# Layer norm kept feature-major, with sums over partitions as f32 matmuls against ones, in an eight-core macaron block on Trainium2

## What is computed

```python
x = x + 0.5 * tanh(layernorm(x) @ W @ A1 @ A2 + bias)
u = layernorm(x)
q, k, v = u @ Wq + bq, u @ Wk + bk, u @ Wv + bv
Q, K = elu(q) + 1, elu(k) + 1
KV, Ksum = sum(K * v, axis=1), sum(K, axis=1)      # over the sequence
V = Q * KV / (Q * Ksum + 1e-6)
x = x + gelu(V @ Wo + bo)
x = x + 0.5 * tanh(layernorm(x) @ W @ A1 @ A2 + bias)
```

## Time and profile before

| quantity | us |
|---|---|
| median of two runs | 3260.82 |
| lowest, highest | 3228.44, 3293.2 |
| profiled execution, its own time | 3213.7 |
| span on its slowest core (core 2) | 3212.1 |
| spans of the eight cores | 3197.8 to 3212.1 |
| mean granted TensorE clock, dies 0 and 1 | 0.790, 0.805 |

### The profile page before, as it was taken

The page is one execution under the profiler, slowest core; times in us unless marked ns, Lnnn a source line. Parts: engine busy times, 40 slices in busy tenths (PEclk is TensorE's granted clock), DMA queues, the critical chain, the costliest instruction groups (busy, mean ns, idle before and its releaser), DMA issues.

```text
span 3212.1 us, 32797 instructions; the slowest of 8 cores (3197.8 to 3212.1 us)
## 1 busy us (share of the span) xinstructions
PE 1953.5 (61%) x10048; PEld 1041.0 (32%) x10048; DVE 1708.4 (53%) x2885; ACT 1491.5 (46%) x1672; POOL 6.5 (0%) x11
## 2 busy tenths in 40 slices
PE   4776555677665556776646566565665755656555
PEld 2443333334333333443223232232332322323222
DVE  2256567665666676555454544544545444454453
ACT  2444444454444444543344444544545545455443
POOL 0000000000000000000000000000000000000000
PEclk9888778788787778887777787777777877778777
DMA  5621221012111111100501110111101111011110
GB/s 112 121 70 40 66 66 54 38 66 66 53 53 66 66 44 49 66 40 37 122 0 66 66 45 22 66 66 66 56 10 66 66 66 66 1 65 66 66 53 27
DMA packets 34572, 184.68 MB, mean 57 GB/s; under 512 B 2528, under 2 KB 2656, under 8 KB 26208
## 3 DMA queue, kind: packets, MB, share of 16 engines
q1 hardware_dynamic: 27120, 167.90, 15.0%
q0 software_dynamic: 7280, 14.68, 2.9%
HBM read 113.36 MB, written 83.89 MB: 61 GB/s over the span
## 4 chain that ended last, share of the span: by engine, by line
PE 50%; DVE 21%; ACT 11%; DVEq 7%; issue 5%; ACTq 4%; DMA 2%; POOL 0%; POOLq 0%; SPq 0%
PE psF L310 42%; DVEq L157 6%; PE psF L377 5%; DVE kk L411 4%; ACTq L157 4%; DVE u_tm L466 3%; ACT ufm L360 3%; DVE u_tm L630 2%; DVE kk L608 2%; DVE vv L612 2%; PE psB L352 2%; PE psF L264 2%; DMA WB<-A 2%; ACT kk L606 2%; ACT xy L387 1%
## 5 line engine op out<-in xcount | busy, mean ns | idle before, releaser
L352 PE MATMUL psB<-ibf,u_tm 128*128 128x128 bf16 x1536 | 145.4, 280 | 651.5 <-DVE statbuf L452 341.9
L310 PE MATMUL psF<-ufm,WA 128*128 128x512 bf16 x2048 | 495.1, 406 | 44.4 <-ACT ufm L360 34.4
L310 PE MATMUL psF<-ufm,Mb 128*128 128x512 bf16 x2048 | 473.6, 394 | 32.3 <-ACT ufm L360 32.3
L310 PE MATMUL psF<-u_tm,WB 128*128 128x512 bf16 x1024 | 260.6, 422 | 309.2 <-DVE u_tm L630 309.2
L360 ACT ACTIVATE ufm<-psB 128x1024 bf16<-128x1024 bf16 x192 | 196.5, 1023 | 409.5 <-PE psB L352 397.9
L352 PEld LDWEIGHTS psB<-ibf,u_tm 128*128 128x128 bf16 x1536 | 136.5, 130 | 668.0 <-issue 664.2
L310 PEld LDWEIGHTS psF<-ufm,WA 128*128 128x128 bf16 x2048 | 208.4, 103 | 316.3 <-issue 136.4
L310 PEld LDWEIGHTS psF<-ufm,Mb 128*128 128x128 bf16 x2048 | 205.1, 101 | 293.9 <-issue 71.6
L310 PEld LDWEIGHTS psF<-u_tm,WB 128*128 128x128 bf16 x1024 | 107.8, 106 | 458.2 <-issue 362.5
L310 PE MATMUL psF<-ufm,WB 128*128 128x512 bf16 x1024 | 224.5, 380 | 0.0
L377 PE MATMUL psF<-i,Y 128*128 128x128 f32 x1024 | 164.6, 310 | 80.9 <-DVE Y L503 48.5
(11 more groups left out here) (89 smaller groups left out, 2448.3 us busy)
## 6 DMA issues: line engine op xcount, KB each, us to landing
xy<-x SPq DMA_DIRECT2D x16, 2048.0 KB, 11.8
y1sp<-Y SPq DMA_DIRECT2D x16, 2048.0 KB, 6.7
Y<-y1sp SPq DMA_DIRECT2D x16, 2048.0 KB, 11.3
out<-xy SPq DMA_DIRECT2D x16, 2048.0 KB, 10.5
u2sp<-ufm SPq DMA_DIRECT2D x16, 1024.0 KB, 5.5
ufm<-u2sp SPq DMA_DIRECT2D x16, 1024.0 KB, 6.2
WB<-A POOLq DMA_DIRECT2D x2, 2048.0 KB, 29.4
WA<-Wt POOLq DMA_DIRECT2D x1, 2048.0 KB, 31.3
```

The costliest lines, as they stand in the source:

```text
L310: ins = t.matmul(out=bank, lhsT=lhs[:, D * k + 128 * mb: D * k + 128 * mb + 128], rhs=rhs[:, 512 * k: 512 * k + 512], start=(k == 0), stop ...
L352: ins = t.transpose(out=bank[:, 512 * ci + 128 * s_: 512 * ci + 128 * s_ + 128], in_=src_tm[:, 1024 * s_ + 128 * c: 1024 * s_ + 128 * c + ...
```

## The change

- `ln_stats`, `normalize` and `tm_to_fm_bf` are gone, with u_tm and the statistics buffers. A new function `fmln` does the layer norm on the fm tile. ScalarE squares it; TensorE sums Y and its square over the partitions by eight f32 matmuls each, with a column of ones (128x1) as the stationary operand and 512 columns moving, into one row of psSx and of psSq; ScalarE copies the two rows to STT; VectorE forms mean and variance on 1x512; ScalarE forms the inverse root as Exp(-0.5 Ln(var)); TensorE broadcasts the inverse root and mean times it to 128 partitions by an f32 matmul with a row of ones; ScalarE copies both to BC; VectorE multiplies and subtracts, chunk by chunk, and writes bf16 to ufm.
- The f32 transposes of Y back to tm before the second and the third layer norm (1024 instructions of L377) and all 1536 bf16 transposes of L352 are gone. The transposes of x into Y, and those of the result before the store, stay.
- In the first loop the first layer norm now reads Y, and uses the x buffer as scratch.
- psB has two banks instead of four; psSx and psSq take the other two.
- In `p1_D` the minimum, Exp, and the two products work on halves of 2048 elements with names of their own. The trees stay whole.
- V in the second loop is written to ufm instead of u_tm.
- Costs of the new operations are written by hand like the others, and the scheduler orders anew. `tree_reduce` and `fm_to_tm` take lists of names; what they compute is the same.

```diff
-    u_tm0 = sb("u_tm0", [128, 4096], BF16).ap()
-    u_tm1 = u_tm0
...
-    statbufs = [sb(f"statbuf{p}", [128, 7 * SUB], F32).ap() for p in range(2)]
+    STT = sb("STT", [128, 2 * 512], F32).ap()
+    BC = sb("BC", [128, 4 * 512], F32).ap()
+    ones_c = sb("ones_c", [128, 1], F32).ap()
+    ones_f = sb("ones_f", [128, 128], F32).ap()
...
-    psB = [nc.alloc_psum_tensor(f"psB{i}", [128, 1024], BF16).ap() for i in range(4)]
+    psB = [nc.alloc_psum_tensor(f"psB{i}", [128, 1024], BF16).ap() for i in range(2)]
+    psSx = nc.alloc_psum_tensor("psSx", [128, 512], F32).ap()
+    psSq = nc.alloc_psum_tensor("psSq", [128, 512], F32).ap()
     psf_free = [None] * 4
-    psb_free = [None] * 4
+    psb_free = [None] * 2
+    pssum_free = [[None, None], [None, None]]
...
+    def fmln(src, src_names, scr, scr_name, dst, dst_name, par):
+        row = 64 * par
+        p = str(par)
+        s0 = STT[row:row + 1, 0:512]
+        s1 = STT[row:row + 1, 512:1024]
+        smq = BC[row:row + 1, 1024 * par: 1024 * par + 512]
+        bc_i = BC[:, 1024 * par: 1024 * par + 512]
+        bc_m = BC[:, 1024 * par + 512: 1024 * par + 1024]
+        onesr = ones_f[row:row + 1, :]
+        ci = cbuf[row:row + 1, 3:4]
+        ce = cbuf[row:row + 1, 1:2]
+        scn = cn(scr_name)
+        dcn = cn(dst_name)
+        B.op("scalar", lambda s: s.activation(out=scr, in_=src, func=AF.Square),
+             reads=list(src_names), writes=[scr_name] + scn, cost=3700.0)
+        def mk_mm(rhsbuf, bank):
+            def f(t):
+                ins = None
+                for k in range(NCH):
+                    ins = t.matmul(out=bank[row:row + 1, :], lhsT=ones_c,
+                                   rhs=rhsbuf[:, 512 * k: 512 * k + 512],
+                                   start=(k == 0), stop=(k == NCH - 1))
+                return ins
+            return f
+        tms = B.op("tensor", mk_mm(src, psSx), reads=list(src_names) + ["ones"],
+                   waits=[pssum_free[0][par]], cost=3000.0)
+        tmq = B.op("tensor", mk_mm(scr, psSq), reads=[scr_name] + scn + ["ones"],
+                   waits=[pssum_free[1][par]], cost=3000.0)
+        ev = B.op("scalar", lambda s: (
+            s.activation(out=s0, in_=psSx[row:row + 1, :], func=AF.Copy),
+            s.activation(out=s1, in_=psSq[row:row + 1, :], func=AF.Copy))[-1],
+            writes=["sx" + p, "sq" + p], waits=[tms, tmq], cost=1500.0)
+        pssum_free[0][par] = ev
+        pssum_free[1][par] = ev
+        B.op("vector", lambda v: v.tensor_scalar(
+            out=s0, in0=s0, scalar1=ci, scalar2=None, op0=ALU.mult),
+            reads=["sx" + p, "consts"], writes=["mean" + p], cost=600.0)
+        B.op("vector", lambda v: v.tensor_tensor(
+            out=smq, in0=s0, in1=s0, op=ALU.mult),
+            reads=["mean" + p], writes=["msq" + p, "bci" + p], cost=600.0)
+        B.op("vector", lambda v: v.scalar_tensor_tensor(
+            out=s1, in0=s1, scalar=ci, in1=smq, op0=ALU.mult, op1=ALU.subtract),
+            reads=["sq" + p, "msq" + p, "consts"], writes=["var" + p], cost=600.0)
+        B.op("vector", lambda v: v.tensor_scalar(
+            out=s1, in0=s1, scalar1=ce, scalar2=None, op0=ALU.add),
+            reads=["var" + p, "consts"], writes=["var" + p], cost=600.0)
+        B.op("scalar", lambda s: s.activation(out=s1, in_=s1, func=AF.Ln),
+             reads=["var" + p], writes=["var" + p], cost=750.0)
+        B.op("scalar", lambda s: s.activation(out=s1, in_=s1, func=AF.Exp,
+                                              scale=-0.5),
+             reads=["var" + p], writes=["istd" + p], cost=750.0)
+        B.op("vector", lambda v: v.tensor_tensor(
+            out=s0, in0=s0, in1=s1, op=ALU.mult),
+            reads=["mean" + p, "istd" + p], writes=["mi" + p], cost=600.0)
+        for which, (sseg, rd, bcout, bwr) in enumerate([
+                (s1, "istd" + p, bc_i, "bci"), (s0, "mi" + p, bc_m, "bcm")]):
+            bi = 2 * par + which
+            bank = psF[bi]
+            tb = B.op("tensor", lambda t, sseg=sseg, bank=bank: t.matmul(
+                out=bank, lhsT=onesr, rhs=sseg, start=True, stop=True),
+                reads=[rd, "ones"], waits=[psf_free[bi]], cost=400.0)
+            tbe = B.op("scalar", lambda s, bank=bank, bcout=bcout: s.activation(
+                out=bcout, in_=bank, func=AF.Copy),
+                reads=[rd], writes=[bwr + p], waits=[tb], cost=750.0)
+            psf_free[bi] = tbe
+        for c in range(NCH):
+            B.op("vector", lambda v, c=c: v.tensor_tensor(
+                out=scr[:, 512 * c: 512 * c + 512],
+                in0=src[:, 512 * c: 512 * c + 512], in1=bc_i, op=ALU.mult),
+                reads=[src_names[c], "bci" + p], writes=[scn[c]], cost=600.0)
+            B.op("vector", lambda v, c=c: v.tensor_tensor(
+                out=dst[:, 512 * c: 512 * c + 512],
+                in0=scr[:, 512 * c: 512 * c + 512], in1=bc_m, op=ALU.subtract),
+                reads=[scn[c], "bcm" + p], writes=[dst_name, dcn[c]], cost=700.0)
...
     def p1_A(idx):
         xy, xyn = xys[idx % 2]
-        t1, t1n = t1s[idx % 2]
+        ufm, ufm_name = ufms[idx % 2]
         B.op("sync", lambda s, idx=idx, xy=xy: s.dma_start(
             out=xy.rearrange("p (sb d) -> p sb d", d=D),
             in_=x_d[idx * TILE:(idx + 1) * TILE, :].rearrange("(sb p) d -> p sb d", p=128)),
-            writes=[xyn], sem=f"sIX{idx % 2}", dma=True, cost=7000.0)
+            writes=[xyn] + cn(xyn), sem=f"sIX{idx % 2}", dma=True, cost=7000.0)
         tm_to_fm_f32(xy, xyn, Y, cn("Y"))
-        ln_stats(xy, xyn, t1, t1n, kk, "kk", idx % 2)
-        normalize(xy, xyn, *utms[idx % 2], idx % 2)
+        fmln(Y, cn("Y"), xy, xyn, ufm, ufm_name, idx % 2)
 
     def p1_B(idx):
         ufm, ufm_name = ufms[idx % 2]
-        u_tm, u_name = utms[idx % 2]
         t1, t1n = t1s[idx % 2]
-        tm_to_fm_bf(u_tm, u_name, ufm, ufm_name)
...
-        fm_to_tm(Y, cn("Y"), vv, "vv")
-        ln_stats(vv, "vv", t1, t1n, kk, "kk", idx % 2)
-        normalize(vv, "vv", u_tm, u_name, idx % 2)
-        tm_to_fm_bf(u_tm, u_name, ufm, ufm_name)
+        fmln(Y, cn("Y"), t1, t1n, ufm, ufm_name, idx % 2)
...
+                   chunk_names=[[f"zkH{j // 4}"] for j in range(NCH)])
         projection(WB, "WB", ufm, ufm_name,
                    lambda s, mb, bank: s.activation(
                        out=vv[:, 512 * mb: 512 * mb + 512], in_=bank, func=AF.Copy),
-                   ["vv"])
+                   [], chunk_names=[[f"vvH{j // 4}"] for j in range(NCH)])
...
+        for h in range(2):
+            kh = kk[:, 2048 * h: 2048 * h + 2048]
+            zh = zk[:, 2048 * h: 2048 * h + 2048]
+            vh = vv[:, 2048 * h: 2048 * h + 2048]
+            KN = [f"kkH{h}"]; ZN = [f"zkH{h}"]; VN = [f"vvH{h}"]
+            B.op("vector", lambda v, kh=kh, zh=zh: v.tensor_scalar(
+                out=kh, in0=zh, scalar1=0.0, scalar2=None, op0=ALU.min),
+                reads=ZN, writes=KN, cost=1100.0)
+            B.op("scalar", lambda s, kh=kh: s.activation(out=kh, in_=kh, func=AF.Exp),
+                 reads=KN, writes=KN, cost=2000.0)
+            B.op("vector", lambda v, kh=kh, zh=zh: v.scalar_tensor_tensor(
+                out=kh, in0=zh, scalar=0.0, in1=kh, op0=ALU.max, op1=ALU.add),
+                reads=ZN + KN, writes=KN, cost=2200.0)
+            B.op("vector", lambda v, kh=kh, zh=zh, vh=vh: v.scalar_tensor_tensor(
+                out=zh, in0=kh, scalar=1.0, in1=vh, op0=ALU.mult, op1=ALU.mult),
+                reads=KN + VN, writes=ZN, cost=2200.0)
...
-        fm_to_tm(Y, cn("Y"), xy, xyn)
-        ln_stats(xy, xyn, t1, t1n, vv, "vv", idx % 2)
-        normalize(xy, xyn, *utms[idx % 2], idx % 2)
+        fmln(Y, cn("Y"), t1, t1n, ufm, ufm_name, idx % 2)
...
```

More of the change, by code:

```diff
@@ L235, in build_program @@
         writes=["consts"])
+    B.op("vector", lambda v: (
+        v.memset(ones_c, 1.0), v.memset(ones_f, 1.0))[-1],
+        writes=["ones"])
     B.op("sync", lambda s: s.dma_start(out=i32, in_=i32_d), writes=["i32"],
@@ L280, in build_program @@
     for ck in range(NCH):
-        bi = ck % 4
+        bi = ck % 2
         bank = psB[bi]
@@ L300, in build_program, with nm @@
     wload(WB, wv_d, "WB")
+    def nm(x):
+        return list(x) if isinstance(x, (list, tuple)) else [x]
+    KKN = ["kk", "kkH0", "kkH1"]
+    ZKN = ["zk", "zkH0", "zkH1"]
+    VVN = ["vv", "vvH0", "vvH1"]
     def projection(lhsT_buf, lhs_name, rhs_buf, rhs_name, evac_fn, evac_writes,
@@ L316, in projection @@
                         waits=[psf_free[bi]], cost=1900.0)
-            wl = [chunk_names[mb]] if chunk_names else list(evac_writes)
+            if chunk_names:
+                cnm = chunk_names[mb]
+                wl = list(cnm) if isinstance(cnm, (list, tuple)) else [cnm]
+            else:
+                wl = list(evac_writes)
             tok_e = B.op("scalar", lambda s, mb=mb, bank=bank: evac_fn(s, mb, bank),
@@ L389, in fm_to_tm @@
```

(13 more changed lines are left out.)

128 lines of the change are left out of this document (26 added, 102 removed).

## The result

| | before | after |
|---|---|---|
| median of the runs, us | 3215.7 | 3317.3 |
| the same over the executions kept, us | 3215.2 | 3316.3 |
| profiled execution, us | 3213.7 | 3315.1 |
| its slowest core, span, us | 3212.1 | 3313.5 |

The ratio of the two is 1.032, with a 95% interval of 1.030 to 1.034: the change makes the kernel slower by 3.2%. The profiled executions differ by 101 us, where the prediction's sum was +24; 3317 lies inside its range of 3100 to 3400 but above the 3164 to 3293 that it gave to the forecast itself. Executions in which one die ran at a lower clock than the other are left out of every ratio and of the times of the experiments; of one experiment (e3_warm) hardly another kind was seen, so no ratio stands with it.

The account below looks back on a forecast made before the run. The layer norm's serial chain was taken as the bound. First loop +84 and second loop -60 made +24 on 3213.7, so 3238; with 12 added for the runs shown, 3250 us, range 3100 to 3400.

Parts of the forecast that it names:

- the prediction's sum: Whole kernel: first loop with start and junction +84, second loop -60, together +24 us on the profiled 3213.7, giving 3238.
- What bounds the kernel: Both loops: the serial chain of the layer norm decides; TensorE stands still 650.8 us before the bf16 transposes.
- The price of an f32 matmul: Layer norm sums: 0.87 us for each f32 matmul with 512 columns, 768 of them.
- the rival of the warm transposes' rate: Layer norm sums: f32 matmuls run at the warm transposes' rate, 269 us less, 2981; chance 0.08.
- the rival that one-column matmuls never bring the clock up: Layer norm sums: matmuls using one array column stay at the lower clock, 668 us more, 3918; chance 0.13.
- The chain's steps: First loop: ufm ready 35.5 us after Y, the next tile's sums end at 45.4; first Y stored at 177.4.
- The rival of a shorter chain: Layer norms: cheaper small steps save 4 us per first-loop tile and 3 per second, -105, 3145; chance 0.17.
- The first loop's period: First loop: 94.7 and 95.0 us in the two kinds of tile, so 95.0 against 92.3 before.
- The first rival, 3361: First loop: after pauses, four sum matmuls of each group cost double at the lower clock, 111 us; chance 0.25.
- The second loop's gain: Second loop: Y to Mb 38.1 us against 41.9, with Mb's clock -4.3 a tile, -64 us over fifteen tiles.
- Start, junction and end: Outside the steady loops: start +37 us, halves at the junction -2, last second-loop tile +4.
- The 12 us put on the sum: Whole kernel: 12 us added because the runs shown were 15 and 47 us above the profile, making 3238 into 3250.

Follow-up runs that it names:

- e3_warm: The kernel after, plus 28 unread bf16 matmuls ahead of the broadcasts of the Y update's layer norm in both loops: 3309.8 to 3577.7 us.
- e11_warm_first: The kernel after, plus 28 unread bf16 matmuls ahead of the broadcasts of the Y update's layer norm, first loop only: 3268.3 us, ratio 1.019.

## Why the prediction was wrong, point by point

- *What bounds the kernel* was right: the layer norm's chain. It still bounds it, in another form, with the sums on TensorE in it instead of VectorE's trees.
- *The price of an f32 matmul*, 0.87, was right: 7.03 us for eight, 0.88. By the Trainium skill, "FP8 and Floating Point Precision", section "TensorE Precision Notes" (four passes), an estimate from four bf16 rows is 0.87; the trace agrees. From the rows alone the hit was luck: they left 0.52 to 0.93, and the transposes whose fourfold was 0.93 ran in part at the lower clock; at the upper one they give 0.52, where the matmuls take 0.88. So the rival of the warm transposes' rate (2981) is out. So is the rival that one-column matmuls never bring the clock up: in the group that starts at 1165.5 the granted clock is 0.50 in 1166 to 1168 and 1.00 in 1170 to 1172, with nothing but sums on TensorE.
- *The chain's steps* came out at their sum: ufm at 36.3 after Y (35.5 forecast), the next tile's sums' end at 45.7 (45.4), first Y at 177.6 (177.4). One step was too cheap, the broadcast, priced 1.3 and taking 2.2 before its copy can start, at the lower clock; the first multiply starts 25.1 us after Y for 23.8, and VectorE's sixteen steps take 11.2 for 11.7. The rival of a shorter chain falls too.
- *The first loop's period*, 95.0, is the step that failed. It was built from projections at the upper clock, 13.98 each and 10.5 for 48 matmuls, and a single "1.0 for a part at the lower clock" in the sums. After's fifteen intervals are 53 us over the forecast's 1425 on core 3 and 25 on core 7. Filling the wait for the statistics, with nothing else changed in the order, takes 51 and 20 us of these away. Core 3's tile from 1064.0 shows where they go, in us after Y: the last broadcasts end at 55.9 (52.9 forecast), the 48 matmuls of WA behind them at 68.5 (63.4), Mb at 96.9 (91.3), and the next Y comes at 101.4 (94.7). The first rival, 3361, had this cause and put it in the wrong instructions: it was to hold from 43 us of slow sums on, and the sums lost 31 (368.5 us busy in psSx and 337.5 in the three psSq groups, against 675 at full rate). The broadcasts and the projections behind them lost the rest.
- *The second loop's gain* was -64 for fifteen tiles and is -41. In half of the tiles Mb waits for Q's 48 matmuls, which were to take 10.5 us and took 13.2 at the lower clock, so up to 39.2 for 37; in the others VectorE's minimum holds it at 39.0, as forecast (39.3). That is about 0.9 of the 1.5 us missed per tile. The rest is Mb itself: the forecast took 0.7 a tile off for its start at the upper clock in half of the tiles, but in the others the wait of 5.8 us lets it take 16.8, so their mean is 15.4, as before. This is read from the traces; no experiment tried it alone.
- *Start, junction and end* were right within 3 us.
- *The sum* was too low because a lower clock behind TensorE's waits was priced in the sums alone. With the 51 us of e11_warm_first and the 23 us that the table has for the second loop, +24 becomes +98, and core 3 shows +103. The 12 us put on the sum for the runs shown had nothing to answer to: before's median turned out 2 us above its profile.
